# Constant products in TensorE's gaps, a reordered prologue, unscaled row transposes and mask tiles among the projections

## The chip, the cores and the metric

One core of a Trainium2 chip runs the kernel. The metric is the time on the device in microseconds (us), lower is better. The engines are TensorE (PE; its weight loads are PEld), VectorE (DVE), ScalarE (ACT), GpSimd (POOL) and SyncE (SP, which issues DMAs). A profile is one execution; its rows are in us from the first instruction.

## The reference

Two layers, each followed by adding its input and a layer norm, on `x` of 2 x 4096 x 256 in f32:

```python
# layer 1: a gated linear recurrence over the sequence
a = tanh(x @ WA.T); b = x @ WB.T                 # 16 states
g = sigmoid(x @ Wg.T + bg); dx = x @ WD.T + bD
h_t = a_t * h_{t-1} + b_t                        # scan over 4096 tokens
x = layernorm(x + (h @ WC.T) * g + dx * (1 - g))
# layer 2: a transformer block on a chosen eighth of the tokens
w = x @ router_w + router_b
sel = sort(the 511 highest w of each batch)      # threshold: the 512th
x_s, pos, m = x[sel], position_ids[sel], mask[sel][:, sel]
hn = rmsnorm(x_s) * ln1
q, k, v = rope(hn @ wq), rope(hn @ wk), hn @ wv  # 16 heads of 16
x1 = x_s + softmax(q k^T / 4 + m) v @ wo
x2 = x1 + gelu((rmsnorm(x1) * ln2) @ w1) @ w2    # w1: 256 x 1024
out[sel] = x2 * w[sel]; out += x * (1 - (w > threshold))
x = layernorm(x + out)
```

## The kernel before

The program is written out by hand: each engine has its own list of instructions in order, and counting semaphores (`wait_ge`, `then_inc`) order them against each other. Nothing is scheduled by a planner; on each engine an instruction waits for all that stand before it.

**Prologue (lines 411 to 427, 709 to 731, 1051 to 1114, 1375 to 1407).** SP loads the first four groups of `x` and the gate weights; ACT issues the loads of WA, WB, three copies of WC side by side, and the biases. All seven weight loads count on one semaphore, `w_loaded`, and PE waits for all of them (line 711) after turning the first half of the first `x` group. PE then transposes WA and WB (line 714) and the tripled WC (line 717) together, then the second half of `x` (line 664), then Wg and WD (line 723). ACT and DVE split each result into a high and a low part for exact-enough fp32r products.

**Layer 1 (lines 732 to 743, 1408 to 1428).** 16 groups of 512 tokens. Per group PE transposes `x` (`transposes`), forms the recurrence inputs (`recurrence_inputs`), and the gates with the h part last (`gates`, lines 689 to 705). ACT does copies, tanh, sigmoid and the final normalisation, DVE the scan (line 1299) and statistics, POOL a subtraction and the powers.

**Selection (lines 745 to 784, 1356 to 1511).** The 512th-highest logit is found digit by digit: `compare` on DVE (line 1360) marks logits at or above 15 candidates, `count` on PE (line 748) sums over the partitions with eight small products of a matrix of ones, `narrow` on DVE takes the digit. Eight rounds per batch, the two batches interleaved. Then `flag_sums`, `slots` (ranks) and `one_hots` (lines 1457 to 1466: a one-hot of the high part of the slot, one of the low part, and the second times 15 values). `pick_rows` multiplies the one-hots to give the row numbers; `pick_rest` does the other 13 values: the factors of each row (`wf_sel`) and positions. `rows` on DVE makes three index tiles and POOL's `gather_x` and `gather_mask_rows` fetch rows of `x` and of the mask by them; POOL waits for all three index tiles (`rows_ready`, 3).

**Projections (lines 819 to 854, 1005 to 1026).** `first_normalised` on DVE (line 1544) multiplies a gathered chunk of 128 rows by its norm factor `wf_sel[..., 2]`; PE transposes it (line 826), ACT copies it to `hnT` (line 1150), PE forms q and k (line 848) and v (line 852), ACT copies q and k out (line 1160), DVE v (line 1562). PE also turns eight 128 x 512 tiles of mask rows per batch (line 797), which ACT negates and copies (line 1170), SP stores and POOL gathers again by column. In PE's list all eight tiles of batch 0 stand between the projections of batch 0 and those of batch 1, and all eight of batch 1 after the first two chunks of batch 1. `turn_split` (line 867) then turns the split q and k.

**Attention and feed-forward, per batch (lines 1028 to 1047).** PE goes through 64 head units (lines 898, 911, 926), then the output product, the transposes of the normalised rows (`turn_hn`, line 834), the hidden layer (lines 978 and 984) and the second product (line 1001). Before `turn_hn` DVE sums squares and POOL takes the power (line 584), and PE has nothing to do. For batch 0, PE turns the second batch's mask columns there (line 816).

The scratch tiles of the selection lie in `qk[0]` (`scratch`, line 228).

## Time and profile before

| | us |
|---|---|
| median of 3 runs (516.37 to 517.21) | 516.37 |
| the profiled execution, its own time | 516.65 |
| its span, first to last instruction | 514.9 |
| PE busy | 428.7 (83%) |
| DVE busy | 393.8 (76%) |
| ACT busy | 289.9 (56%) |
| POOL busy | 173.5 (34%) |

The 1.75 us between the execution's own time and its span lie outside the instructions. The clock column of the profile (PEclk) is the TensorE clock that was granted, as a share of 2.4 GHz; 0.5 is 1.2 GHz, the lower of its two levels. The mean over the span is 0.934.

### The profile page before, as it was taken

What the parts mean: (1) busy time and instruction counts of PE and PEld (TensorE: products, weight loads), DVE (VectorE), ACT (ScalarE), POOL (GpSimd) and SP (SyncE); (2) the same over time, 40 slices, a digit from 0 to 9 for tenths busy, and PEclk for the clock granted to TensorE, in tenths of its full rate; (3) what the DMA queues carried; (4) which work ended last, traced back from release to release, by engine and by line L of the source; (5) the groups of instructions that cost most, each with busy time, mean ns of one, the idle gap of its engine ahead of it and who ended that gap; (6) DMA issues with size and microseconds to landing.
All of it is one profiled execution on the core that took longest, in us unless ns stands there. A gap on an engine that the chain in (4) does not pass through costs nothing.

```text
span 514.9 us, 9944 instructions
## 1 busy us (share of the span) xinstructions
PE 428.7 (83%) x3394; PEld 326.8 (63%) x3394; DVE 393.8 (76%) x1218; ACT 289.9 (56%) x613; POOL 173.5 (34%) x210
## 2 busy tenths in 40 slices
PE   3598999998999723589887999997998999996970
PEld 2487888776888512457565666665885666664860
DVE  1777898789888788777468999978667999967150
ACT  2344655554465534014687999964577999962200
POOL 9146757756775750354234000001000000000532
PEclk9999999998999955579999999998999999998995
DMA  8613252243222120056670000000000000000110
GB/s 250 215 43 83 83 158 89 81 137 110 81 83 83 41 82 1 26 181 210 237 232 16 3 3 1 3 2 1 0 1 2 2 2 3 2 2 1 35 37 11
DMA packets 29913, 33.90 MB, mean 66 GB/s; under 512 B 6404, under 2 KB 25512, under 8 KB 29864
## 3 DMA queue, kind: packets, MB, share of 16 engines
q1 hardware_dynamic: 23088, 24.78, 14.6%
q0 software_dynamic: 3520, 8.40, 5.5%
q10 hardware_dynamic: 3256, 0.10, 0.4%
q8 instruction: 27, 0.44, 0.4%
q14 instruction: 22, 0.18, 0.1%
HBM read 19.63 MB, written 13.63 MB: 65 GB/s over the span
## 4 chain that ended last, share of the span: by engine, by line
PE 37%; DVE 14%; issue 14%; POOL 9%; ACT 5%; POOLq 1%; DVEq 0%; ACTq 0%
PE ps L911 8%; PE ps L926 5%; PE ps L898 4%; PE ps L1001 4%; PE ps L978 3%; POOL arena L499 3%; PE ps L848 2%; PE ps L867 2%; PE ps L762 2%; POOL r L508 2%; ACT arena L1207 1%; PE ps L984 1%; POOL h_parts L558 1%; POOL rq L513 1%; PE ps L852 1%
## 5 line engine op out<-in xcount | busy, mean ns | idle before, releaser
L1207 ACT ACTIVATE arena<-arena,nmax 128x511 f32<-128x511 f32 x128 | 91.5, 719 | 5.4 <-DVE nmax L1643 5.3
L1643 DVE CUSTOM_DVE_ANT_0 arena<-ps,nmask 128x511 f32<-128x511 f32 x128 | 84.8, 684 | 0.2 <-DVE nmask L1591 0.2
L911 PE MATMUL ps<-ident,arena 128*128 128x128 f32 x512 | 78.7, 276 | 3.6 <-ACT big L403 2.3
L911 PEld LDWEIGHTS ps<-ident,arena 128*128 128x128 f32 x512 | 58.7, 140 | 25.3 <-ACT arena L1207 15.1
L689 PE MATMUL ps<-wgd_hi,x_hi 128*128 128x512 f32 x128 | 51.6, 403 | 0.0
L691 PE MATMUL ps<-wgd_hi,x_lo 128*128 128x512 f32 x128 | 50.5, 394 | 0.0
L690 PE MATMUL ps<-wgd_lo,x_hi 128*128 128x512 f32 x128 | 50.3, 393 | 0.0
L898 PE MATMUL ps<-arena 96*128 96x512 bf16 x128 | 48.5, 385 | 1.9 <-DVE nmask L1591 1.1
L403 DVE COPY big<-ps 128x512 f32<-128x512 f32 x64 | 44.1, 689 | 4.8 <-PE ps L911 3.6
L499 POOL TENSOR_TENSOR arena<-arena 128x512 f32<-128x512 f32 x32 | 41.4, 1294 | 12.4 <-DVE arena L1311 10.8
L403 ACT COPY big<-ps 128x512 f32<-128x512 f32 x64 | 36.9, 577 | 8.0 <-PE ps L926 6.3
L1094 ACT ACTIVATE ob_sb<-arena,nb,rq 128x256 f32<-128x256 f32 x64 | 33.1, 591 | 8.6 <-POOL nb L517 8.5
L1286 DVE TENSOR_TENSOR x_lo<-ps,x_hi 128x512 fp32r<-128x512 f32 x32 | 22.0, 688 | 15.5 <-ACT x_hi L1065 15.5
L664 PE MATMUL ps<-ident,arena 128*128 128x128 f32 x128 | 20.9, 289 | 12.5 <-DVE x_lo L1286 7.6
L1065 ACT CAST x_hi<-ps 128x512 fp32r<-128x512 f32 x32 | 18.6, 580 | 21.2 <-PE ps L664 20.9
L1306 DVE TENSOR_TENSOR arena<-ps,arena 128x512 f32<-128x512 f32 x32 | 21.9, 685 | 10.2 <-PE ps L705 10.1
L1077 ACT ACTIVATE arena<-ps 128x512 f32<-128x512 f32 x32 | 19.2, 599 | 18.0 <-PE ps L698 16.0
L1086 ACT CAST h_parts<-arena 48x512 fp32r<-48x512 f32 x16 | 9.9, 621 | 33.2 <-DVE arena L1299 33.2
L631 POOL COPY arena<-v_sb 128x256 f32<-128x256 f32 x4 | 1.6, 397 | 80.2 <-PE ps L926 80.2
L1001 PE MATMUL ps<-w_sb,big 128*128 128x256 f32 x128 | 28.6, 380 | 0.0
L1319 DVE BATCH_NORM_STATS2 stats<-arena 128x6 f32<-128x256 f32 x64 | 23.9, 415 | 5.8 <-POOL arena L499 5.8
L508 POOL TENSOR_TENSOR r<-v,minus_half 128x8 f32<-128x8 f32 x16 | 26.3, 1643 | 5.9 <-DVE v L1336 5.9
(243 smaller groups left out, 1005.0 us busy)
## 6 DMA issues: line engine op xcount, KB each, us to landing
arena<-in_L_attn_x SPq DMA_DIRECT2D x16, 512.0 KB, 4.6
out<-ob_sb SPq DMA_DIRECT2D x16, 512.0 KB, 3.2
w_sb<-in_L_ffn_w SPq DMA_DIRECT2D x2, 1024.0 KB, 10.3
mt_scratch<-nmask SPq DMA_DIRECT2D x8, 256.0 KB, 4.9
mt_scratch<-big SPq DMA_DIRECT2D x8, 256.0 KB, 4.4
big<-in_L_attn_Wg SPq DMA_DIRECT2D x1, 256.0 KB, 4.2
big<-in_L_attn_WD SPq DMA_DIRECT2D x1, 256.0 KB, 5.5
wqk<-in_L_ffn_wq SPq DMA_DIRECT2D x1, 256.0 KB, 7.7
```

The source lines that it names most:

```text
L403: copy(prT[c % 2][:, h, :, :], ps[:, 2 + u % 2, :].rearrange("p (k n) -> p k n", k=C)).then_inc(prT_copied[u % 2], 1)
L499: pool.tensor_tensor(s, s, u_sb[q][:, :, :], ALU.subtract).then_inc(s_ready, 1)
L508: pool.tensor_tensor(r2[:, :, b, n], v2[:, :, b, n], minus_half[:, 0:2 * T].rearrange("p (k t) -> p k t", k=2), ALU.pow).then_inc(r2_ready, 1)
L689: pe.matmul(o, hi, wgd_hi[:, c, :], start=(c == 0), stop=False)
L690: pe.matmul(o, hi, wgd_lo[:, c, :], start=False, stop=False)
L691: pe.matmul(o, lo, wgd_hi[:, c, :], start=False, stop=False)
L898: pe.matmul(ps[:, S_BANKS[u % AHEAD], :], qkT[0][:, hg * HG + h:hg * HG + h + 1, c * P:(c + 1) * P], qkT[1][:, hg * HG + h:hg * HG + h + 1 ...
L911: mm = pe.transpose(ps[:, 2 + u % 2, k * P:(k + 1) * P], pr[u % 4][:, k * P:(k + 1) * P], ident[:, :])
L1001: mm = pe.matmul(second_out(b, c), hidden_sb[:, f, c * P:(c + 1) * P], w2_sb[:, f, :], start=(f == 0), stop=(f == FB - 1))
L1094: last = act.activation(ob_sb[G % 2][:, t, :], s_sb[G % 2][:, t, :], ACT.Identity, bias=nb[G % 2][:, t:t + 1], scale=rq[:, b, n.start + t: ...
L1207: act.activation(pr[u % 4][:, 0:K - 1], sm[u % 4][:, 0:K - 1], ACT.Exp, bias=nmax[:, c, h:h + 1], scale=-1.0, accum_out=rsum[:, c, h:h + 1 ...
L1643: dve.tensor_tensor_reduce(sm[u % 4][:, 0:K - 1], ps[:, S_BANKS[u % AHEAD], 0:K - 1], nmask[b][:, c, 0:K - 1], 1.0, 3.4e38, ALU.add, ALU.m ...
```

## The change

`fill(bank, n)` is new on PE: n products of a matrix of ones with 512 constant columns into a bank that nobody reads. 14 smaller ones stand in the prologue. The loads get a semaphore each; WC is loaded once and tripled by a DVE copy; PE takes WA and WB as soon as they are there and WC after the first recurrence inputs. ACT makes a one-column copy at the start and issues the bias loads after its first copy of `x`. In `one_hots` the two values that `pick_rows` needs come first. POOL waits for one index tile at a time. `first_normalised` is gone: PE transposes the gathered rows as they are, and the factor is applied in the copies of q, k and v. The mask tiles of batch 0 are dealt out 3, 2, 3 among the first projections of batch 1, and banks are given out anew (`X_BANK`, three banks for mask tiles). The scratch tiles move to `v_sb[1]` and `x_sel[1]`.

```diff
@@ scratch tiles, banks
-            return early_qk[:, at:at + n].bitcast(dt)
+            tile, at = (v_sb[1], at) if at < 992 else (x_sel[1], at - 992)
+            return tile[:, :, :].rearrange("p c d -> p (c d)")[:, at:at + n].bitcast(dt)
-        R_BANK, REST_BANK = (2, 0), (4, 1)
+        R_BANK, REST_BANK = (2, 0), (1, 1)
+        X_BANK = ((2, 3), (3, 3))
@@ POOL
-            pool.wait_ge(rows_ready[0], 3)
...
             def kept(b):
-                pool.wait_ge(hn_ready[b], C)
+                pool.wait_ge(angle_ready[b], 1)
                 for c in range(C):
+                    pool.wait_ge(x_sel_in[b][c], 16)
...
-            gather_x(0)
-            gather_mask_rows(0)
-            pool.wait_ge(rows_ready[1], 3)
-            gather_x(1)
-            gather_mask_rows(1)
-            gather_mask_columns(0)
-            gather_mask_columns(1)
+            for b in range(B):
+                pool.wait_ge(rows_ready[b], 1)
+                gather_x(b)
+                pool.wait_ge(rows_ready[b], 2)
+                gather_mask_rows(b)
+            for b in range(B):
+                pool.wait_ge(rows_ready[b], 3)
+                gather_mask_columns(b)
@@ PE
+            ones_wide = ones_b[:, :].rearrange("p (o n) -> p o n", o=1).broadcast_to((P, 4, P))
+            def fill(bank, n):
+                for _ in range(n):
+                    pe.matmul(ps[:, bank, :], ones_b[:, :], ones_wide, start=True, stop=True)
...
             pe.wait_ge(ident_ready, 2)
+            ident_bits = ident[:, :].bitcast(BF16)
+            for n in range(10):
+                pe.matmul(ps[:, 7, 0:2 * P], ident_bits[:, 0:P], ident_bits, start=True, stop=True)
             transposes(0, 0)
-            pe.wait_ge(w_loaded, 16 * 7)
+            pe.wait_ge(wab_loaded, 16 * 2)
...
-            for h in range(2):
-                mm = pe.transpose(ps[0:HROWS, 5, h * P:(h + 1) * P], wc_raw[:, h, :], ident[:, :])
-            mm.then_inc(wt_done, 1)
+            mm.then_inc(w_turned, 1)
+            for n in range(4):
+                pe.matmul(ps[:, 7, 0:2 * P], ident_bits[:, 0:P], ident_bits, start=True, stop=True)
             transposes(0, 1)
+            pe.wait_ge(wgd_loaded, 16 * 2)
...
             pe.wait_ge(split_ready, KD)
             recurrence_inputs(0)
+            pe.wait_ge(split_ready, KD + 1)
+            for h in range(2):
+                mm = pe.transpose(ps[0:HROWS, 5, h * P:(h + 1) * P], wc_raw[:, h, :], ident[:, :])
+            mm.then_inc(w_turned, 1)
             for c in range(KD):
                 transposes(1, c)
...
             def pick(b, lo, hi, bank, at, signal):
-                pe.wait_ge(lo_ready[b], 1)
+                pe.wait_ge(lo_ready[b], 1 if hi == 2 else 2)
...
             def pick_rest(b):
+                if b > 0:
+                    pe.wait_ge(angle_ready[b - 1], 1)
                 pick(b, 2, VALS, REST_BANK[b], 0, rest_picked)
 
-            for r in range(4):
+            pe.wait_ge(pool_const, 9 + 2 * B)
+            pe.wait_ge(t_ready, 2 * NGB)
+            fill(7, 6)
+            for r, gap in enumerate((13, 10, 4, 7)):
                 count(0, r)
+                fill(7, gap)
             for r in range(4, ROUNDS):
                 count(1, r - 4)
+                fill(7, 2)
                 count(0, r)
+                fill(7, 2)
             count(1, 4)
+            fill(7, 1)
             flag_sums(0)
+            fill(7, 2)
             count(1, 5)
+            fill(7, 13)
             count(1, 6)
+            fill(7, 12)
             pick_rows(0)
             count(1, 7)
             pick_rest(0)
             flag_sums(1)
+            fill(7, 12)
...
             def turn_first_hn(b, c):
-                pe.wait_ge(hn_ready[b], c + 1)
-                if c + b * C >= 2:
-                    pe.wait_ge(hnT1_ready[(c + b * C - 2) // C], (c + b * C - 2) % C + 1)
-                if b > 0:
-                    pe.wait_ge(mT_ready[b - 1], MS // P)
+                pe.wait_ge(x_sel_in[b][c], 16)
+                if b == 0 and c >= 2:
+                    pe.wait_ge(hnT1_ready[0], c - 1)
+                elif b == 1:
+                    pe.wait_ge(hnT1_ready[1], c)
...
-            turn_mask_rows(0)
-            for c in range(2):
+            turn_mask_rows(0, range(3))
+            turn_first_hn(1, 0)
+            project(1, range(1))
+            turn_mask_rows(0, range(3, 5))
+            turn_first_hn(1, 1)
+            project(1, range(1, 2))
+            turn_mask_rows(0, range(5, 8))
+            for c in range(2, C):
                 turn_first_hn(1, c)
-            for c in range(2):
-                project(1, range(c, c + 1))
-                turn_first_hn(1, 2 + c)
-            turn_mask_rows(1)
+            turn_mask_rows(1, range(8))
+            pe.wait_ge(v_ready[1], 2)
+            fill(7, 10)
+            pe.wait_ge(hnT1_ready[1], C)
             pe.wait_ge(mT_ready[1], MS // P)
...
                 if b == 0:
                     turn_second_mask_columns()
-                    pe.wait_ge(nm_ready[1], 2)
+                    pe.wait_ge(nm_ready[1], C)
+                    fill(5, 5)
+                else:
+                    fill(5, 14)
                 turn_hn(b)
@@ ACT
-            for r in range(3):
-                act.dma_start(wc_raw[:, :, r * N:(r + 1) * N], WC.rearrange("(h e) n -> e h n", e=P)).then_inc(w_loaded, 16)
-            act.wait_ge(bias_zeroed, 1)
...
+            act.dma_start(wc_one[:, :, :], WC.rearrange("(h e) n -> e h n", e=P)).then_inc(wc_loaded, 16)
+            act.wait_ge(ident_ready, 3)
+            act.copy(nb[0][:, 0:1], minus_half[:, 0:1])
...
             copy_xT(0, 0)
+            load_biases()
             copy_xT(0, 1)
-            act.wait_ge(wt_done, 1)
-            act.copy(wc_hi[:, :], ps[0:HROWS, 5, 0:D]).then_inc(wt_copied, 1)
             for c in range(KD):
...
+            act.wait_ge(w_turned, KD + 2)
+            act.copy(wc_hi[:, :], ps[0:HROWS, 5, 0:D]).then_inc(w_hi_ready, 1)
...
             def copy_qk(b, c):
-                act.copy(qk[b][:, c, :], ps[:, 4 + c % 2, :]).then_inc(qk_ready[b], 1)
+                act.wait_ge(angle_ready[b], 1)
+                act.mul(qk[b][:, c, :], ps[:, 4 + c % 2, :], wf_sel[:, b, c, 2:3]).then_inc(qk_ready[b], 1)
...
-            sines(0)
             for c in range(2):
                 copy_first_hnT(0, c)
+            sines(0)
...
             copy_qk(0, C - 1)
+            copy_mask_rows(0, range(3))
+            copy_first_hnT(1, 0)
+            copy_qk(1, 0)
+            copy_mask_rows(0, range(3, 5))
+            copy_first_hnT(1, 1)
+            more_parts(0, 0)
+            copy_qk(1, 1)
+            copy_mask_rows(0, range(5, 8))
+            for c in range(2, C):
+                copy_first_hnT(1, c)
+            copy_mask_rows(1, range(5))
+            more_parts(0, 1)
+            copy_mask_rows(1, range(5, 8))
             sines(1)
...
@@ DVE
             rest_of_x(0, 0)
-            dve.wait_ge(wt_done, 1)
+            dve.wait_ge(w_turned, 1)
...
-            rest_of_x(0, 1)
             for m in range(2):
...
+            rest_of_x(0, 1)
+            dve.wait_ge(wc_loaded, 16)
+            dve.tensor_copy(wc_raw.rearrange("p h (r n) -> p h r n", r=3),
+                            wc_one.rearrange("p h (r n) -> p h r n", r=1).broadcast_to((P, 2, 3, N))).then_inc(split_ready, 1)
...
             def one_hots(b):
-                dve.tensor_tensor(at_hi[:, b], slot_b[:, b, 0:1, :].broadcast_to((P, P, NT)), hi_rep[:, :, :],
-                                  ALU.is_equal).then_inc(at_ready[b], 1)
                 step.link(dve.tensor_tensor(
                     at_lo[:, b], slot_b[:, b, 1:2, :].broadcast_to((P, C, NT)),
...
+                place(0, 2)
+                dve.tensor_tensor(at_hi[:, b], slot_b[:, b, 0:1, :].broadcast_to((P, P, NT)), hi_rep[:, :, :],
+                                  ALU.is_equal).then_inc(at_ready[b], 1)
                 dve.wait_ge(parts_ready[b], 1)
+                place(2, VALS)
...
             def value(b, c):
                 dve.wait_ge(v_done[b], c + 1)
-                dve.tensor_copy(v_sb[b][:, c, :], ps[:, 6 + c % 2, 0:D]).then_inc(v_ready[b], 1)
+                dve.tensor_scalar(v_sb[b][:, c, :], ps[:, 6 + c % 2, 0:D], wf_sel[:, b, c, 2:3], None,
+                                  ALU.mult).then_inc(v_ready[b], 1)
```

`place(v0, v1)` multiplies the low one-hot by the values v0 to v1 - 1 and signals `lo_ready`. The calls of `first_normalised` are removed from DVE's list.

## Rows read from the trace of the kernel before

**Rows 1.** The page, slices of the whole span (one slice is 12.9 us).

```profile
PE   3598999998999723589887999997998999996970
...
PEclk9999999998999955579999999998999999998995
```

**Rows 2.** Busy us by stretch: length, PE, PEld, DVE, ACT, POOL, clock, DMA share, GB/s.

```profile
181.00:225.00 44.00, 18.37 (x196) 14.09 (x197) 36.99 (x172) 11.01 (x20) 14.93 (x19) 0.50 0.19 61
354.00:358.00 4.00, 3.95 (x13) 2.85 (x14) 3.90 (x12) 2.33 (x3) 0.15 (x1) 0.57 0.01 4
470.00:474.00 4.00, 4.00 (x13) 2.88 (x14) 2.65 (x7) 2.46 (x3) 0.00 (x0) 0.57 0.02 4
239.70:258.10 18.40, 14.27 (x89) 10.64 (x88) 11.05 (x28) 13.86 (x32) 3.97 (x5) 1.00 0.75 254
```

**Rows 3.** The timeline of 0 to 25 us: start, duration, engine, line, operation.

```profile
4.84 1.09 PE L664 MATMUL ps<-ident,arena 128*128 128x128 f32 x4 [4.84 <-DMA arena<-in_L_attn_x]
...
5.12 1.28 ACT L1065 ACT_TABLE_LOAD   x1 [5.12 <-issue]
...
7.03 0.69 DVE L1286 TENSOR_TENSOR x_lo<-ps,x_hi 128x512 fp32r<-128x512 f32 x1 [3.71 <-ACT x_hi L1065]
...
9.94 0.61 PE L714 MATMUL ps<-ident,nmask 16*128 16x16 f32 x4 [4.01 <-DMA nmask<-in_L_attn_WC]
...
11.74 1.71 PE L723 MATMUL ps<-ident,big 128*128 128x128 f32 x8
...
14.47 0.50 PE L675 MATMUL ps<-x_hi,wab_hi 128*128 128x512 f32 x1 [1.02 <-DVE wab_lo L1383]
...
14.81 0.40 PE L676 MATMUL ps<-x_lo,wab_hi 128*128 128x512 f32 x1
...
17.85 1.27 DVE L1299 TENSOR_TENSOR_SCAN arena<-arena,zero_state,ps 48x512 f32<-48x512 f32 x1
...
23.14 0.70 PE L698 MATMUL ps<-wc_d,h_parts 128*128 128x512 f32 x2 [1.67 <-DVE wc_d L1402]
```

**Rows 4.** DMA issues of 0 to 20 us: KB each, median us to landing.

```profile
nmask<-in_L_attn_WC ACTq DMA_DIRECT2D x3, 16.0 KB, 6.1
...
nmask<-in_L_attn_WB ACTq DMA_DIRECT2D x1, 16.0 KB, 3.7
```

**Rows 5.** The timeline of 197 to 215 us, selection.

```profile
197.03 0.58 PE L748 MATMUL ps<-arena,ones_b 128*128 128x60 bf16 x8 [0.70 <-DVE arena L1360]
...
198.10 0.58 PE L748 MATMUL ps<-arena,ones_b 128*128 128x60 bf16 x8 [0.48 <-DVE arena L1360]
...
206.15 2.28 DVE L1458 TENSOR_TENSOR arena<-slot_b,qk 128x4096 bf16<-128x4096 bf16 x1
...
208.66 1.16 DVE L1464 TENSOR_TENSOR arena<-at_lo,qk 128x1920 bf16<-128x1920 bf16 x1
...
209.88 2.22 PE L762 MATMUL ps<-arena 128*128 128x8 bf16 x32 [3.02 <-DVE arena L1464]
...
214.00 1.22 POOL L579 DMA_INDIRECT x_sel<-out,row_x  x1 [22.89 <-DVE row_t L1477]
```

**Rows 6.** The timeline of 220 to 259 us, projections and mask tiles.

```profile
220.94 1.12 PE L826 MATMUL ps<-ident,hn 128*128 128x128 f32 x4 [5.05 <-DVE hn L1544]
...
222.19 3.22 PE L848 MATMUL ps<-wqk,hnT 128*128 128x512 f32 x4
...
231.26 1.88 PE L848 MATMUL ps<-wqk,hnT 128*128 128x512 f32 x4
...
254.03 4.02 ACT L1170 ACTIVATE big<-ps 128x512 f32<-128x512 f32 x8
...
258.10 1.99 PE L867 MATMUL ps<-ident_b,arena 128*96 128x128 bf16 x32 [1.29 <-ACT big L1170]
```

**Rows 7.** The timeline of 469 to 476 us, before the second feed-forward.

```profile
469.92 2.12 PE L834 MATMUL ps<-ident,hn 128*128 128x128 f32 x8 [3.77 <-DVE hn L1537]
...
474.79 1.09 PE L984 MATMUL ps<-hnT_lo,w_hi 128*128 128x512 f32 x4
```

More of the change, by code:

```diff
@@ L241, in build @@
         rope_a, rope_b = (arena2[:, n * 1024:(n + 1) * 1024].rearrange("p (c n) -> p c n", c=2) for n in range(2))
-        v_sb = [sb(f"v_sb{b}", [P, C, D]) for b in range(B)]
         e_rest = arena2[:, 4096:5120].rearrange("p (e n) -> p e n", e=2)
@@ L1246, in _ @@
             copy_qk(0, C - 1)
-            sines(1)
-            copy_mask_rows(0)
-            for c in range(2):
-                copy_first_hnT(1, c)
-            more_parts(0, 0)
-            for c in range(2):
-                copy_first_hnT(1, 2 + c)
-                copy_qk(1, c)
-            more_parts(0, 1)
-            copy_mask_rows(1)
+            copy_mask_rows(0, range(3))
[11 more added lines that the diff above has]
+            copy_mask_rows(1, range(5, 8))
+            sines(1)
             for c in range(C):
@@ L1724, in _ @@
             slots(1)
-            for c in range(2):
-                first_normalised(0, c)
             one_hots(1)
-            for c in range(2, C):
-                first_normalised(0, c)
             cosines(0)
@@ L1740, in _ @@
                     parts(0, 0)
-                if c == 2:
-                    for n in range(C):
-                        first_normalised(1, n)
             parts(0, 1)
```

86 lines of the change are left out of this document (43 added, 43 removed).

## The prediction

> **What bounds the kernel now.** I read the slices of the page first, for the clock: it is at 0.5 in one long stretch, 181 to 225 us, and falls for a moment near 126, 355 and 471 us; PE shows nines nearly everywhere else [rows 1]. The busy times by stretch then say who works where. In layer 1 PE is full, so what starts earlier in the prologue is kept to the end. In 181 to 225 us PE is busy 18.4 of 44 us at clock 0.50 while DVE is busy 37.0: the selection is DVE's [rows 2]. Next the timeline at its start, for what PE waits on: it stands 4.01 us for a DMA of WC [rows 3], which is three small loads of 6.1 us each, the last issued on ACT's queue behind WA and WB [rows 4]. Then the timeline of the selection and of the projections, for the chain one-hots, picked rows, gather, normalised rows, transposes [rows 5, 6], and last the gap before the second feed-forward [rows 7].
>
> All of it is worked against the profiled execution: 516.65 us (span 514.9), 0.28 above the median of 516.37.
>
> **Part 1, prologue.** WB takes 3.7 us against 6.1 for WC [rows 4], so with a semaphore of their own WA and WB (first on ACT's queue) are there when the first transposes end, at 4.84 + 1.09 = 5.9 us. ACT's 1.28 us table load, which ran at 5.12 to 6.4 and held up the first copy, goes to ACT's empty time ahead of 4.8 by the one-column copy: 0.4 us. The first rest of x ended at 7.03 + 0.69 = 7.7; now about 7.3, and the second half of `x`, which was turned just ahead of the transposes at 11.74, is turned then, 3.5 us earlier [rows 3]. From there: transposes to 8.4, ACT's copy to 9.05 (0.6), DVE's rest to 9.8 (0.69). The WA/WB split (about 1.1 us in four small DVE operations) now runs while PE turns `x`; before it stood behind the rest of x and released line 675 at 14.47. Wg and WD are turned meanwhile (1.71 us at most), to 10.1. So line 675 starts near 10.1: 4.4 us earlier. Given back: the two WC transposes and their copy now stand between that and the second group (about 0.6). The scan at 17.85 becomes 14.1, the h part of the first gates at 23.14 becomes 19.4, if the bias loads, now issued on ACT behind its first copy (from 6.5 instead of 3.5 us), land before about 17.5. Sum -3.7. Bounds: 0 (a load I moved is late and takes the whole of it) and -4.4. ACT's four bias issues, some 1.6 us, fit between its copies at 6.5 and 8.4; the tripling copy on DVE is about 0.2 us, beside PE.
>
> The row that bears on the clock: from 9.94 to 13.3 us PE ran transposes and nothing else; they came 0.21 us apart (8 in 1.71), which is the low level, and at 14.81 the products last 0.40 as they do later at the full one [rows 3]. So transposes alone raised the clock here. The Trainium skill (TensorE: Matmul & The Clock Gate, Part 4: PE-mode transpose) says that the full clock does not engage for transposes; the trace does not agree. By that rule only the 14 small products would count and the first recurrence inputs would run at half clock, a rival below.
>
> **Part 2, products that fill gaps.** No row shows one; the nearest is line 984: four of 512 columns in 1.09 us of which the last alone is 0.40, so (1.09 - 0.40) / 3 = 0.23 us each at full clock [rows 7], 0.46 at the low one. In the count rounds two counts are 1.07 us apart and PE idles 0.48 of that [rows 5]. One count (0.58 low, about 0.4 full) and two fills (0.46) take 0.86 at full clock: nothing waits, and nothing is gained either, since DVE sets the pace; at the low clock they take 1.50 and are late by 0.43. The runs of 13, 12 and 12 are 3.0, 2.8 and 2.8 us; the idle they fill ahead of count(1,6) and of the picked rows is about 3.3 and 3.0 [rows 5]. The six ahead of the first count (1.4 us from 178.4) delay it by some 0.5 us, and DVE reads it 2 us later. I take 0 for the lot, bounds -0.3 and +1.0; what a warm clock gives comes in part 4.
>
> **Part 3, one-hots and index tiles.** The big one-hot takes 2.28 us, the values 1.16, then the pick starts at 209.88 [rows 5]. Now only 2 of 15 values stand ahead: 1.16 x 13/15 = 1.0 less, one more operation (0.3) more; the pick starts 0.7 earlier, near 209.2. POOL's gather at 214.00 waited for the third index tile, row_t; two small DVE operations (0.35) less. First gather near 212.9, -1.1. The other 13 values run on DVE beside the pick (2.2 us) and cost nothing.
>
> **Part 4, rows transposed unscaled, warm.** The first transposes at 220.94 waited for DVE, which did angles and slots before it scaled the rows [rows 6]; the rows themselves are there by 212.9 + 1.2 + some 3 = 217. Now PE takes them when its 12 fills end, near 217.9. Projection 0 took 3.22 for its first part at the low clock against 1.88 at the full one, 1.3 less [rows 6]. So the first chunk is done 4.5 us earlier; then PE waits for the second batch's one-hots on DVE, whose list is eight scalings shorter but was never waiting for PE, and the last chunk of batch 0 ends about 236.6 instead of 239.7: -3.1. Scaling in the copies is the same operation with a factor: 0, bounds -0.1 and +0.1 each over 16. The added waits: `copy_qk` waits for the angles, which DVE has some 3 us before the first q and k and 5 us before those of batch 1 (behind it on ACT stand the next hnT copies, for which PE would wait); `pick_rest(1)` waits for the angles of batch 0, long done; POOL's `kept` waits for rows that PE has turned by then. All 0.
>
> **Part 5, mask tiles.** From the last copy of batch 0 to the end of the tiles (239.7 to 258.1) ACT is busy 13.9 of 18.4 us [rows 2]; its last eight tiles, 0.50 each, end what `turn_split` at 258.10 waits for [rows 6]. ACT's list is the same work in another order, plus the second batch's sines. It waits 4.5 us now. In the new order it waits for projection (1,0), which stands behind three tiles (2.1), for tiles 3 and 5 behind projections (0.7, 0.5), for the first tile (0.7) and little else; with the last three tiles behind `more_parts` I get about 5.4. So of the 3.1, 2.2 are left: `turn_split` at 255.9. The ten fills there (2.3 us) end near 255.1, under ACT's tiles. Stores of batch 0 end some 4 us later than now, but its columns are gathered well before PE wants them near 270. Bounds: +1 and -3.5. What follows to 275 us is unchanged.
>
> **Part 6, feed-forwards.** Batch 1: PE is idle 3.77 us up to 469.92, then 4 us at clock 0.57 [rows 2, 7], that is 4 x 0.43 = 1.7 us lost. 14 fills are 3.2 us, they end before 469.9. The transposes are still held by DVE's rows and ACT's copy; I take -1.3, bounds 0 and -1.7. Batch 0: five fills (1.2 us) start only when ACT has copied the last mask tile, 353.9, so `turn_hn` starts about 1 us later, against a low clock over 354 to 358 [rows 2]. If the clock holds, -0.4; if it falls all the same, +1.5. I take 0.
>
> **Sum.** -3.7 - 2.2 - 1.3 = -7.2 on 516.65: 509.45, and 0.28 less for the median, 509.2. Attention and layer 1 are PE bound and unchanged.
>
> **Rivals.**
> A. The prologue is held by another load (biases, or the one WC): parts 2 to 6 alone, 512.9. For: WC's loads took 6.1 us each against 3.7 for WB, so the queues are full there [rows 4]; against: every load but the biases moves forward. Chance 0.12.
> B. The middle keeps its end, since ACT waits longer among interleaved tiles: 511.4. For: ACT ends last there; against: everything ahead of it is 3 us earlier. 0.15.
> C. The prologue runs at the low clock until after the first recurrence inputs: six products at 0.43 instead of 0.23, +1.4, 510.6. The row on transposes speaks against it. 0.13.
> D. Slower: constant products do not hold the clock in the selection. It decides from the first long gap, 180 us on: eight rounds late by 0.43 (3.4), 13 and 12 fills at 0.46 against gaps of 3.3 and 2.3 (2.7 and 3.2), 12 after the flag sums (2.5), 14 at 466 (2.7), five at 354 (1.5): +16, less the prologue's 3.7 and 0.7 of part 3, 528. For: no row shows what such a product does to the clock; against: every stretch in which PE is dense has clock 1.0. 0.06; smaller mishaps of this kind that end above before 0.02.
> E. Gains and losses cancel: 516.4. 0.04.
> The forecast itself has 0.48, with its own range 507.5 to 510.3.
>
> **How the numbers follow.** Within 0.2% (515.3 to 517.4) is what a measurement of this kernel can't tell from no change. Faster: 0.48 + 0.12 + 0.15 + 0.13 = 0.88; same 0.04; slower 0.08. The range leaves out D and E and reaches to A: 505.8 to 513.4.
>
> **What would show it.** Right: line 675 starts near 10.1, the h part of the first gates near 19.4; PEclk is 1.0 from 180 to 260; the first gather starts near 212.9 - 3.7, `turn_split` near 255.9 - 3.7; clock 1.0 at 470. Wrong: PE's count waits for nothing while DVE waits for it in the rounds (D); line 698 waits for a DMA (A); ACT's tiles end at 254 or later (B).

## The result, and the profile after

| | before | after |
|---|---|---|
| median, in turn on the same chip | 516.79 (4 runs, 516.37 to 517.92) | 510.54 (4 runs, 509.67 to 513.3) |
| the profiled execution, its own time | 516.65 | 513.3 |
| its span | 514.9 | 511.4 |
| PE busy | 428.7 | 457.1 |
| mean granted clock | 0.934 | 0.97 (0.97 to 0.98 over the four) |

The ratio of the two kernels' runs is 0.9867 (95% interval 0.9839 to 0.9895), that of the two medians alone 0.9879: the kernel after is 1.2 to 1.3% faster. 509.2 was forecast, with 505.8 to 513.4 as the range. The profiled execution is the slowest of the four, 2.8 above the median, so all that it shows is read beside the others below.

The page's slices of the kernel after (40 of the whole span, 12.8 us each) are to be held against [rows 1]:

```profile
PE   7698999997999877998997999998998999998970
...
PEclk9899999999999999799999999998999999999995
```

The long stretch of fives is gone, and a 7 is left at slice 17. The windows of the kernel after, in the columns of [rows 2], say where the clock is still low:

```profile
22.00:24.00 2.00, 0.91 (x5) 0.94 (x6) 1.29 (x2) 1.97 (x3) 0.00 (x0) 0.74 0.01 4
24.00:26.00 2.00, 2.00 (x6) 1.61 (x6) 1.36 (x2) 0.72 (x2) 0.98 (x1) 0.50 0.00 0
...
177.00:210.00 33.00, 26.59 (x248) 12.88 (x249) 28.21 (x134) 10.19 (x19) 8.49 (x13) 1.00 0.10 33
210.00:217.90 7.90, 7.90 (x46) 4.92 (x46) 5.49 (x34) 0.00 (x0) 5.03 (x6) 0.57 0.22 67
218.00:260.00 42.00, 38.53 (x259) 27.89 (x258) 25.92 (x68) 24.05 (x50) 16.53 (x15) 1.00 0.69 228
...
351.00:354.00 3.00, 3.00 (x11) 1.86 (x10) 2.90 (x10) 0.08 (x1) 0.00 (x0) 0.50 0.00 0
...
470.00:474.00 4.00, 3.78 (x17) 2.81 (x16) 3.93 (x13) 2.31 (x3) 0.00 (x0) 1.00 0.00 0
```

The selection (177 to 210) runs at 1.00 where it had 0.50. New falls stand at 23 to 26 and at 210 to 217, and the one before the first feed-forward has moved from 354 to 351. At 470, where 0.57 stood, it is 1.00. A fall near 126 us is in both kernels and costs nothing that shows: "no five" below has it and "both" has not, and their first compares stand at 175.78 and 175.77.

The timeline of the kernel after, 0 to 21 us, against [rows 3]:

```profile
8.31 4.16 POOL L483 IOTA qk<- 128x4096 bf16 x1
...
8.55 1.91 PE L738 MATMUL ps<-ident,big 128*128 128x128 f32 x8
...
9.41 0.69 DVE L1335 TENSOR_TENSOR x_lo<-ps,x_hi 128x512 fp32r<-128x512 f32 x1 [0.84 <-ACT x_hi L1108]
...
10.02 2.53 DVE L1435 COPY nmask<-nmask 128x96 f32<-128x96 f32 x1
10.25 0.77 PE L686 MATMUL ps<-x_hi,wab_hi 128*128 128x512 f32 x1
10.27 2.28 DVE L1439 TENSOR_TENSOR wgd_lo<-ps,wgd_hi 128x512 fp32r<-128x512 f32 x2
...
10.81 0.63 PE L687 MATMUL ps<-x_lo,wab_hi 128*128 128x512 f32 x1
...
12.52 0.48 PE L688 MATMUL ps<-x_hi,wab_lo 128*128 128x512 f32 x1
...
12.84 0.38 PE L746 MATMUL ps<-ident,nmask 128*48 128x128 f32 x2
...
14.93 1.27 DVE L1348 TENSOR_TENSOR_SCAN arena<-arena,zero_state,ps 48x512 f32<-48x512 f32 x1
...
20.21 0.70 PE L709 MATMUL ps<-wc_d,h_parts 128*128 128x512 f32 x2 [1.65 <-DVE wc_d L1455]
```

The recurrence inputs start at 10.25 (before: 14.47), but the middle four last 0.63 each, the low level. The copy that triples WC, which I had at 0.2, takes 2.53 and ends with POOL's iota (8.31 + 4.16 = 12.47).

The timeline of the kernel after from the selection to the projections, against [rows 5, 6]:

```profile
196.50 0.40 PE L767 MATMUL ps<-arena,ones_b 128*128 128x60 bf16 x8 [0.23 <-DVE arena L1409]
196.74 0.59 PE L666 MATMUL ps<-ones_b 128*128 128x512 bf16 x2
197.57 0.39 PE L767 MATMUL ps<-arena,ones_b 128*128 128x60 bf16 x8 [0.24 <-DVE arena L1409]
...
204.91 2.75 PE L666 MATMUL ps<-ones_b 128*128 128x512 bf16 x12
207.50 2.26 PE L781 MATMUL ps<-arena 128*128 128x8 bf16 x32
...
211.34 1.22 POOL L583 DMA_INDIRECT x_sel<-out,row_x  x1 [21.81 <-DVE row_t L1535]
...
213.20 4.87 PE L666 MATMUL ps<-ones_b 128*128 128x512 bf16 x12
217.91 0.60 PE L857 MATMUL ps<-ident,x_sel 128*128 128x128 f32 x4
218.85 1.96 PE L879 MATMUL ps<-wqk,hnT 128*128 128x512 f32 x4 [0.33 <-ACT hnT L1194]
...
234.46 0.69 ACT L1205 ACTIVATE qk<-ps,wf_sel 128x512 f32<-128x512 f32 x1 [5.21 <-PE ps L879]
...
254.70 1.96 PE L898 MATMUL ps<-ident_b,arena 128*96 128x128 bf16 x32 [0.32 <-issue]
```

The counts are faster (0.40 for 0.58) and still 1.07 us apart: DVE sets the pace. Twelve constant products take 2.75 at full clock (0.23 each) and 4.87 behind the flag sums, nearly all of them at the low one.

The timeline of the kernel after, before each feed-forward, against [rows 7]:

```profile
350.71 2.31 PE L666 MATMUL ps<-ones_b 128*128 128x512 bf16 x5 [2.15 <-ACT nmask L1317]
352.82 1.63 PE L865 MATMUL ps<-ident,hn 128*128 128x128 f32 x8
...
463.77 3.19 PE L666 MATMUL ps<-ones_b 128*128 128x512 bf16 x14
467.70 1.55 PE L865 MATMUL ps<-ident,hn 128*128 128x128 f32 x8 [0.74 <-DVE hn L1595]
...
471.53 1.10 PE L1015 MATMUL ps<-hnT_lo,w_hi 128*128 128x512 f32 x4
```

**The stages side by side.** From each trace I took seven landmarks: the first `compare`, the turning of the split q and k, the last copy of the head outputs and the first GELU of each batch, the last scatter. The table has the us between them, one profiled execution per kernel:

| stage | before | after | again | no product | gap | no five | both | both, tiles together |
|---|---|---|---|---|---|---|---|---|
| 1 to first compare | 178.86 | 177.49 | 176.94 | 176.24 | 175.60 | 175.78 | 175.77 | 175.81 |
| 2 to split q, k | 79.24 | 77.21 | 77.15 | 76.90 | 77.58 | 76.63 | 76.58 | 76.00 |
| 3 attention 0 | 89.19 | 89.38 | 89.39 | 89.96 | 89.39 | 89.38 | 89.97 | 89.53 |
| 4 to first GELU, batch 0 | 12.24 | 13.22 | 13.28 | 12.63 | 13.18 | 11.83 | 11.82 | 11.84 |
| 5 to end of attention 1 | 103.89 | 103.90 | 103.89 | 103.90 | 103.90 | 103.88 | 103.88 | 103.89 |
| 6 to first GELU, batch 1 | 12.04 | 11.00 | 11.00 | 12.26 | 11.00 | 10.99 | 11.00 | 11.00 |
| 7 to last scatter | 26.98 | 26.96 | 26.98 | 26.97 | 26.98 | 26.95 | 26.96 | 26.98 |
| own time | 516.65 | 513.30 | 512.75 | 512.94 | 511.73 | 509.74 | 509.93 | 509.02 |

The kernel after won 1.37 in stage 1, 2.03 in stage 2 and 1.04 in stage 6, and lost 0.98 in stage 4 and 0.19 in stage 3.

### The profile page after: what moved, and what is told of

It reads as the page before. It is cut to its first block, busy times and chain, and to the rows that moved or that the text cites. A ratio compares the mean times of both kernels' runs of the same rounds, so it can differ in the third digit from the quotient of the medians.

```text
span 511.4 us, 10221 instructions
## 1 busy us (share of the span) xinstructions
PE 457.1 (89%) x3533; PEld 336.6 (66%) x3533; DVE 393.8 (77%) x1213; ACT 290.8 (57%) x614; POOL 173.4 (34%) x210
## 4 chain that ended last, share of the span: by engine, by line
PE 46%; DVE 12%; POOL 9%; issue 7%; ACT 6%; POOLq 1%; DVEq 0%; ACTq 0%
PE ps L942 11%; PE ps L957 7%; PE ps L929 6%; PE ps L1032 4%; POOL arena L503 3%; PE ps L1009 3%; PE ps L879 3%; PE ps L666 2%; PE ps L898 2%; PE ps L781 2%; POOL r L512 2%; PE ps L905 1%; ACT arena L1252 1%; PE ps L1015 1%; POOL h_parts L562 1%
## 5 line engine op out<-in xcount | busy, mean ns | idle before, releaser
L666 PE MATMUL ps<-ones_b 128*128 128x512 bf16 x125 | 33.6, 409 | 3.0 <-ACT nmask L1317 2.1
```

What stands on the lines that cost most here:

```text
L666: pe.matmul(ps[:, bank, :], ones_b[:, :], ones_wide, start=True, stop=True)
```

## The experiments

Twelve kernels ran: the kernel after once more, and eleven edits of it. Each left one trace, so a stage's time is that of one execution. The first four shared a chip (kernel before there: 517.63), the next four another (518.16), the last four a third (517.87). The kernel after, unchanged, ran only on the first of these chips.

**The kernel after, unchanged** ("again").

> The changed kernel itself, once more, as the reference of the others on this chip and as a second profile. In the first profile (execution of 513.3 us, the slowest of four; the others 509.7 to 511.2) the clock fell at 23 us, just after the start of layer 1, and the second scan came 12.36 us after the first against 10.86 before: 1.5 us of the prologue's 2.9 lost. Theory 1 (chance): whether the clock falls there differs from one execution to the next; a profile near 510 us shows the two scans about 10.9 apart, and executions spread by 2 to 4 us. Theory 2 (fixed): the new prologue makes the clock fall there always; every profile shows 12.4.

Median 512.26 (509.89 to 514.59), ratio 0.9903 (0.9869 to 0.9937). Unchanged, the same program took anything from 509.7 to 514.6 (both sets together), and the mean clock goes along in part: 0.977 at 509.89, 0.970 or 0.971 at the three slowest. It can't be all of it, as 512.75 and 514.59 both have 0.970, and the kernel before took from 515.7 to 519.8 on this chip at 0.934 every time. The fall at 23 us is in this trace too, that at 351 as well: theory 2 is not refuted here. That part of each is chance, the next runs show.

**No constant product at all.**

```diff
-                for _ in range(n):
+                for _ in range(0):
```

and likewise for the 14 small ones of the prologue.

> The changed kernel without any of the added products (none in the prologue, the selection, before the split or before the feed-forwards); order, waits and loads stay. Theory 1 (order carries most): fills give the second feed-forward 1.0 and the first projection 0.7 to 1.3 and take 1.0 in the first feed-forward, so this is 0.5 to 2 us slower than the changed kernel, near 511.5. Rival (the clock carries most of the gain): it loses 4 us or more and ends at 514 or above. The clock is 0.5 from about 180 to 223 us again, and the pace of the counts stays at 1.07 us.

Median 514.57 (512.85 to 517.65, 12 runs), ratio 0.9955 (0.9931 to 0.9979). So of the 5.4 us that the kernel after was ahead on this chip (517.63 to 512.26), about 2.3 hang on the products and 3.1 on the order of the work; the intervals of the two ratios just overlap (0.9931 and 0.9937 are their inner ends), so the split is rough. It lies between theory 1 (0.5 to 2) and the rival (4 or more). Where? The stage from the first compare to the split is not slower without them: 76.90, against 77.15 in "again". This window of the run without products shows DVE busy 18.2 of 20 us while PE is at 0.50:

```profile
188.00:208.00 20.00, 8.22 (x115) 6.44 (x116) 18.23 (x84) 6.45 (x10) 0.41 (x2) 0.50 0.08 27
```

Against the execution of "no five" below (509.74), in which the clock held nearly throughout, the run without products loses 0.46 in stage 1, 0.27 in stage 2, 0.58 in stage 3, 0.80 in stage 4 and 1.27 in stage 6, 3.4 in all, against 3.2 in their own times. The 0.58 of stage 3 is no work of the products: the clock fell at 272 us in this run, and it did so in "both" below too, which has all of them and takes 89.97 there. The largest piece is the second feed-forward; the 106 products between 177 and 254 us, most of the 125 of this kind, bring 0.3.

**The prologue of before under the rest of after.** PE, ACT and DVE have the old order up to the first recurrence inputs.

> The changed kernel with the prologue of before (one semaphore for seven loads, WC loaded three times, table load late, bias issues first, old order on PE and DVE, no products there); all the rest changed. Theory 1: the prologue is worth the 2.9 us that the first scan came earlier, less what the clock's fall at 23 us costs, so this takes 1.5 to 3 us more than the changed kernel: 512 to 513.5. Rival: the prologue's gain is all given back in layer 1 (the clock), then the same time within 0.5 us.

Median 514.08 (511.89 to 517.61), ratio 0.9932 (0.9907 to 0.9957): the new prologue is worth 1.8 us against the unchanged kernel on that chip, inside theory 1's 1.5 to 3, though the intervals overlap. The first recurrence input is at 14.22, the scan at 17.58. The profiled execution is the slowest of nine (517.61), and the clock fell in it at 24.4 us, for twice as long as in "after": its first compare is at 181.11, later than before. So the fall at the start of layer 1 is not the new prologue's own.

**Products in the gaps of the first group** ("gap").

```diff
+                if G == 0 and q == 0:
+                    pe.wait_ge(pool_const, 2)
+                    fill(7, 6)
                 if G == 0:
                     pe.wait_ge(split_ready, 2 * KD + 2)
...
+                if G == 0:
+                    pe.wait_ge(h_ready, 1)
+                    fill(2, 5)
                 if G + 2 < NGB:
                     transposes(G + 2, 1)
```

> The changed kernel with six more constant products after the first group's gate products (PE waits there 1.7 us for the constants) and five before the second half of group 2 is turned (1.5 us idle). Theory 1 (those two idles let the clock fall at 23 us in some executions): it stays 1.0 from 13 to 120 us, the second scan comes 10.9 us after the first in every profile, the median falls by 0.5 to 1.5 us and the spread shrinks. Rival (the fall has nothing to do with these gaps): same median, or 0.3 us more for products that are late.

Median 509.99 (509.56 to 511.76), ratio 0.9862 (0.9834 to 0.989), 2.3 below the unchanged kernel on the same chip (the intervals overlap a little), where theory 1 gave 0.5 to 1.5. In the windows of this run the clock holds where it had fallen:

```profile
22.00:24.00 2.00, 1.59 (x10) 1.07 (x8) 1.35 (x3) 1.97 (x3) 0.00 (x0) 1.00 0.06 15
24.00:26.00 2.00, 2.00 (x10) 1.61 (x9) 1.68 (x3) 0.98 (x2) 1.20 (x1) 1.00 0.00 0
```

and the first two scans are 10.83 us apart, against 12.22 for the unchanged kernel. In "after" and "again", and in the two runs below with four products and with the tiles together, PE waited for the h part and for x with nothing to do (1.72 busy of 18 to 22 us in "again") and the clock fell; in the five kernels with products in these gaps it did in none. In "no product", "no five" and "early" it held without them. So whether it falls is chance, and the products seem to take the chance away; five traces against seven make that likely and no more. The times say the same: none of the 14 executions of "gap", "both" and "both, tiles together" took over 511.8, while 10 of the 28 of "after", "again", "no five", "early" and the first run with the tiles together took over 512.

**Batch 0 without its five products** ("no five").

```diff
-                    pe.wait_ge(nm_ready[1], C)
-                    fill(5, 5)
+                    pe.wait_ge(nm_ready[1], 2)
```

> Batch 0's feed-forward starts as in the kernel before: the five products are gone and PE waits for two mask tile copies, not four. Theory 1: the five products cost what they take at the low clock, because it falls while PE waits for ACT's last tile copy and they start after that. Last output product of batch 0 to first GELU is 13.2 us after the change and 12.2 before; here 12.2 to 12.4, time -0.9 us. Theory 2: the wait for the last tile copy is what costs, and the products themselves little: with only the products gone this was 12.6, so here again 12.2, but of the 1.0 us 0.4 belongs to the wait and 0.6 to the products. The two give the same time here and are told apart by this run beside the one without any products. Rival: the later start of the transposes is hidden by DVE's and ACT's chain on the normalised rows: stays at 13.2, time the same.

Median 510.3 (509.74 to 513.54), ratio 0.9877 (0.9842 to 0.9913). Stage 4 took 11.83, less than the 12.2 that both theories gave, as the clock did not fall in this stage at all. Theory 2's 0.4 for the wait is out by another trace: in "no product", which waits for all four tile copies, the transposes start 6.75 behind the last copy of the head outputs, as they do before. The rest, 12.63 there for 12.24, goes with its fall, which comes 1.1 later and so lies less over the transposes and more over the hidden layer.

**The five products earlier** ("early").

```diff
-                    pe.wait_ge(nm_ready[1], C)
-                    fill(5, 5)
+                    pe.wait_ge(ms_ready, 1)
+                    fill(0, 5)
+                    pe.wait_ge(nm_ready[1], 2)
```

> In batch 0 the five products stand ahead of PE's wait for the normalised rows (they start when the sum of squares' inputs are there) and not behind the wait for the last mask tile copy. Theory 1: they fill the idle time, the clock does not fall at 350.6 and the transposes and the hidden layer run at 1.0: last output product to first GELU 11.0 to 11.6 as in batch 1 after the change (11.0), against 13.2; time -1.6 to -2.2 us. Rival 1: the clock falls all the same (the second batch's mask columns turned there are no dense work), then 12.2 to 12.4, -0.9. Rival 2: the transposes are bound by DVE's rows, and nothing changes but the clock: 12.6, -0.6.

Median 509.91 (509.65 to 513.2), ratio 0.9872 (0.9836 to 0.9908). The timeline of this run:

```profile
347.17 1.25 PE L666 MATMUL ps<-ones_b 128*128 128x512 bf16 x5 [0.54 <-DVE ms L1579]
348.90 1.60 PE L865 MATMUL ps<-ident,hn 128*128 128x128 f32 x8 [0.48 <-DVE hn L1596]
```

The products sit in the gap and stage 4 takes 11.83 again. It took 11.83 in a third run too, the next one, which has the five products where the kernel after has them. So 11.83 is what the stage takes at full clock, wherever the products stand. What the products decide is the price of a fall: 12.24 (before) and 12.63 (no product) without them, 13.22, 13.28 and 13.18 with five behind it, since they run at 0.46 each in front of the transposes. Whether "early" keeps the clock up or only had luck, its one trace cannot say. The last four runs, all with it, showed no fall there either: none in five traces, against seven in the nine others.

**Four products, not twelve, behind the second flag sums.**

```diff
-            fill(7, 12)
+            fill(7, 4)
```

> Four constant products behind the second batch's flag sums, not twelve. In the kernel after they took 4.87 us at clock 0.5 (213.2 to 218.07) and the gathered rows were transposed at 217.9. Theory 1: they hold PE while the rows are there: the first transposes start at 215.5 to 216 (counted in that run's time), the first chunks 1.5 to 2 us earlier; at the end of the projections 0.5 to 1.0 us is left, as PE then waits for the second batch's one-hots on DVE. Time -0.7. Rival: with fewer products the clock stays at 0.5 longer (it rose to 1.0 just behind the twelve), projection 0 takes 3.2 and not 1.9 us, and nothing is left or 0.5 us is lost. Theory 3: the rows arrive only at 217.5 and nothing changes.

Median 514.07 (512.12 to 514.82), ratio 0.9916 (0.9885 to 0.9946): slower than the three other kernels on this chip by 3.2 to 4.2 us, where theory 1 gave -0.7 and the rival 0.5 at most. The clock fell at 22 us here too, for 6.8 us (stage 1: 178.44). The rows are transposed 3.53 behind the first gather instead of 6.57, but stage 2 takes 79.27:

```profile
222.04 2.19 PE L781 MATMUL ps<-arena 128*128 128x8 bf16 x32 [2.01 <-DVE arena L1521]
224.09 3.76 PE L879 MATMUL ps<-wqk,hnT 128*128 128x512 f32 x4
```

PE comes early to the second batch's one-hot, waits 2.01, the clock falls, and a projection takes 3.76 for 1.96. How much of this is the edit's doing is asked again below.

**Batch 0's mask tiles together**, ahead of batch 1's projections, as before; rows still transposed unscaled.

```diff
-            turn_mask_rows(0, range(3))
-            turn_first_hn(1, 0)
-            project(1, range(1))
-            turn_mask_rows(0, range(3, 5))
-            turn_first_hn(1, 1)
-            project(1, range(1, 2))
-            turn_mask_rows(0, range(5, 8))
+            turn_mask_rows(0, range(8))
+            for c in range(2):
+                turn_first_hn(1, c)
+                project(1, range(c, c + 1))
```

ACT's copies follow.

> The mask tiles of batch 0 stand together ahead of batch 1's projections, as in the kernel before; rows are still transposed unscaled. Theory 1: dealing them out is what makes the middle shorter: without it ACT has no work beside PE's transposes and projections of batch 1 and eight tiles at the end: first compare to turning of the split q and k 79 us against 77.15, time +1.5 to +2. Theory 2 (part 4 of the prediction, and its part 5, where dealing out gives 0.9 back): the gain of 2.0 comes from the rows turned earlier, and the order itself costs or is nothing: 76.3 to 77.2, time -0.8 to 0.

Median 510.92 (510.15 to 514.01), ratio 0.9868 (0.9839 to 0.9896). Stage 2 took 77.39, with the clock at 0.90 over 230 to 234 and 0.68 over 234 to 238, where "after" has 1.00. Theory 1 (79) is out, though this trace can't say what the order costs at an even clock.

**Both gap edits** ("both": "gap" and "early" together), then each of the last three edits on top of it, so that the falls elsewhere do not blur them.

> The kernel after with both edits that kept PE at work in a gap: six and five constant products at the start of layer 1, and batch 0's five ahead of the wait for the normalised rows. Theory 1: what spread the executions of the kernel after (509.7 to 514.6) is whether the clock falls at 23 us (worth 1.5) and at 351 us (worth 1.4); where it held at both, the profiled execution took 509.74. Here it holds at both: 509.6 to 510.0 in nearly all executions, highest below 511. Rival: other falls that no profile has shown make the upper level (513.2 in two of six of the run before, 511.7 in two of five), and it stays: median near 510, highest above 511.5.

Median 510.14 (509.77 to 510.74), ratio 0.985 (0.9816 to 0.9885). The level did not get below the best executions of the kernel after (509.67), but the spread shrank from 4.7 us over six runs ("again") to 1.0 over four. That is theory 1, except that two of the four lie above the 509.6 to 510.0 that it gave for nearly all. Four executions are few, and the low clock doesn't explain every slow one: in "early" 513.20 and 513.18 stand at a mean clock of 0.975, beside 509.93 at 0.977.

> As the kernel with both gap edits, with four products and not twelve behind the second batch's flag sums. In the run with four, PE then waited 2.01 us for DVE's one-hot at 220 us and the clock fell from 223 to 230: the stretch from first gather to the turning of the split q and k took 45.4 us against 43.3. Theory 1: that is the edit's own doing (PE gets to the wait earlier, so the wait is longer), and it shows again: time +2 against the kernel with both gap edits. Rival: it was the chance of one execution: the difference is within 0.5, as the six executions' median of 514.07 came from the two other places where the clock falls.

Median 511.37 (510.6 to 512.44), ratio 0.9876 (0.9848 to 0.9905): +1.2 against "both", so the twelve seem worth having (six executions against four, intervals overlapping; theory 1 gave 2, the rival 0.5), but by another place than I expected. PE waited only 0.75 at 219 us; the clock fell behind the second `pick_rest`:

```profile
226.87 3.42 PE L787 MATMUL ps<-arena 128*128 128x52 bf16 x32
230.11 3.38 PE L885 MATMUL ps<-wqk,hnT 128*128 128x512 f32 x4
```

The clock fell within a few us of there in the first kernel with the tiles together, in the one with the old prologue and in the last run below too, all three with the twelve, and not in "both" or "after", which run the same products there: the earlier arrival makes a fall likelier at best.

> As the kernel with both gap edits, with batch 0's mask tiles together ahead of batch 1's projections. With the kernel after this stretch took 43.6 us against 43.3 (one execution each). Theory 1: the order is worth 0.3 us at most. Rival (dealing out is the gain of the middle): +1.5 to +2.

Median 509.57 (509.02 to 510.44), ratio 0.9842 (0.9812 to 0.9872), the lowest median of all versions. Stage 2 is 0.58 shorter than in "both", with a fall of equal length in each, and the medians are 0.57 apart. The profiled executions are 0.91 apart; 0.44 of that is stage 3, where the clock fell in "both". So dealing the tiles out gains nothing and seems to cost half a microsecond, with the sign of theory 1 turned round; the executions of the two overlap (509.77 to 510.74 and 509.02 to 510.44). Against the kernel after's 0.9867 the intervals overlap; the medians of the two (on different chips) are 1.0 apart.

> As the kernel with both gap edits, with POOL's 4.16 us iota of the high one-hot's pattern moved from the prologue (8.3 to 12.5 us) to the end of layer 1. Theory 1: DVE's copy that triples WC took 2.53 us and the low part of Wg and WD 2.28 (1.28 for two of them in the kernel before) because POOL works beside them; without it the copy takes 0.2 to 0.5 and the low part 0.64 to 1.3. The first recurrence inputs wait for neither, so the first scan stays at 14.7; the first gates are held by other work and the time changes by 0 to -0.5. Rival: the DVE operations are long for their own sake (the copy reads with a stride of zero), and stay. Rival 2: the first gates wait for them, time -1.

```diff
-            pool.iota(hi_rep[:, :, :], [[1, P], [0, NT]], ...).then_inc(pool_const, 1)
...
+                if G == NGB:
+                    pool.iota(hi_rep[:, :, :], [[1, P], [0, NT]], ...).then_inc(hi_made, 1)
```

Median 511.57 (511.46 to 513.65), ratio 0.9874 (0.984 to 0.9909): 1.4 slower than "both", where theory 1 gave 0 to -0.5 (four executions each; those of the two don't overlap). Its timeline has both ends of the matter:

```profile
9.84 0.20 DVE L1444 COPY nmask<-nmask 128x96 f32<-128x96 f32 x1
...
10.09 0.69 DVE L1448 TENSOR_TENSOR wgd_lo<-ps,wgd_hi 128x512 fp32r<-128x512 f32 x1
...
12.32 0.38 PE L751 MATMUL ps<-ident,nmask 128*48 128x128 f32 x2
...
14.42 1.27 DVE L1357 TENSOR_TENSOR_SCAN arena<-arena,zero_state,ps 48x512 f32<-48x512 f32 x1
...
184.46 4.17 POOL L573 IOTA qk<- 128x4096 bf16 x1
...
184.87 3.79 DVE L1402 TENSOR_SCALAR Wf<-Wf,rb_col 128x32 f32<-128x32 f32 x1
```

In the prologue the copy takes 0.20 for 2.53 and the low parts 0.69 each, as theory 1 had it. The scan comes at 14.42 and the first compare at 175.18, which is 0.6 earlier than in "both" and 3.68 earlier than before. (Theory 1 left the scan at 14.7; that miss is answered by the next block.) But the iota in its new place holds an operation of DVE for 3.79 us (184.87 + 3.79 = 188.66; the iota ends at 188.63) that takes 0.29 in "both":

```profile
185.47 0.29 DVE L1400 TENSOR_SCALAR Wf<-Wf,rb_col 128x32 f32<-128x32 f32 x1
```

The first gather comes 37.2 behind the first compare instead of 33.8. The place was badly chosen; the cause is shown twice.

"Both" adds what the low clock had hidden. In its trace the recurrence inputs ran at the full level:

```profile
9.36 3.19 DVE L1442 COPY nmask<-nmask 128x96 f32<-128x96 f32 x1
...
9.59 0.47 PE L686 MATMUL ps<-x_hi,wab_hi 128*128 128x512 f32 x1 [0.62 <-DVE x_lo L1342]
9.90 0.39 PE L687 MATMUL ps<-x_lo,wab_hi 128*128 128x512 f32 x1
...
12.60 0.40 PE L749 MATMUL ps<-ident,nmask 128*48 128x128 f32 x2 [1.39 <-DVE wgd_lo L1446]
```

They ended at 11.2, 1.8 us earlier than in "after" (12.52 + 0.48), and the scan still came at 14.71: PE waited 1.39 for DVE, which the iota held until 12.5. In all eleven traces with this prologue and the iota in it the copy ends at 12.54 or 12.55, though it starts anywhere from 9.36 to 10.15. What the prologue is worth with neither the iota nor the low clock, no run shows: with the iota away the first inputs ran at the low level to the fourth of the six.

## Why the prediction was right

The median is 1.3 above the forecast, well inside the range; most of the mechanism is as predicted. That the sum comes so near is partly luck, as its terms missed in both directions.

- **Part 1** (-3.7). Line 675's products came at 10.25 (forecast near 10.1), no load was late (rival A is out: line 709, the former 698, waits for DVE). The h part came at 20.21, not 19.4: -2.9. The failed step is "the tripling copy on DVE is about 0.2 us, beside PE": it took 2.53 to 3.19, and with the iota away, the first compare moved by -3.68. Rival C (whose price is 6 x 0.20 = 1.2 and not the 1.4 given) happened in part: in the profiled execution the first inputs ran at the low level to the last of the six. But the scan was at 14.71 or 14.72 in nine traces with this prologue, whether full speed began with the first product ("no five", "both") or with the fifth ("again"), as the copy was the later of the two; only here (14.93) and without the small products (15.18) did the low level show. That transposes alone can raise the clock stands: in the trace of before the last two of the eight at line 723 (11.74 to 13.45) take 0.32 and 0.27, the others 0.42. But when they do is no sure thing: in "no product" PE transposed from 7.49 to 10.1 without a gap and all six inputs behind it were still at the low level.
- **What part 1 left out.** Layer 1 keeps what the prologue wins only if the clock stays up. In the profiled execution it fell at 23 us, which made the first two scans 12.36 apart instead of 10.86, so 1.37 of 2.92 was left. That gap was already in the kernel before, and the clock held in its profiled execution (1.00 over 22 to 30). This is the largest piece by which the profiled execution (513.30) lies above the forecast; what it is of the median's 1.3, no run shows.
- **Part 2** (0). Right: 0.23 us a product, first compare to first gather 33.85 with them and 33.97 without. The step "PEclk is 1.0 from 180 to 260" failed between 210.7 and 217.5: the clock fell during the picks and the twelve products took 4.87, not the 2.8 given. Rival D, which was to end at 528, is out. What was said against it, that the clock is 1.0 wherever PE is dense, did not hold in [rows 2] already: 3.95 of 4.00 us busy at 0.57 over 354 to 358.
- **Part 3** (pick -0.7, gather -1.1). Measured from the first compare: pick start 31.02 before, 30.01 after (-1.0); gather 35.14 and 33.85 (-1.3).
- **Part 4** (last copy of q and k of batch 0, -3.1). 60.2 before, 57.0 after, from the first compare: -3.2. The copies with a factor took 0.69 for 0.59 (q, k) and 0.48 for 0.42 (v), inside the bounds.
- **Part 5** (turning at -2.2). -2.03, and -2.61 in "no five", so rival B is out. The share that dealing out gives back was put at 0.9; "both" with the tiles together shows 0.58, one trace against one.
- **Part 6** (batch 1 -1.3, batch 0 taken as 0 with -0.4 and +1.5 as its ends). Batch 1 gave -1.04. Batch 0 had both ends: -0.41 where the clock held, +0.98 where it fell.

In the execution of "no five" (509.74), where neither fall occurred, the stages differ from before by -3.08, -2.61, +0.19, -0.41 and -1.05: -6.9, beside the forecast's -7.2. Its terms there are +0.6 (part 1), -0.4 (part 5), -0.4 (batch 0), +0.25 (batch 1) and +0.19 (stage 3, of which the forecast said that it is unchanged; it is longer in every trace, and why stays open). The median of the kernel after lies 0.8 above this execution. The two falls, each in some executions and not in others, are the likely reason; as only profiled executions show where the clock fell, it is not shown.

The Trainium skill (SBUF — State Buffer, Who interferes with whom) has the rule that I had not applied: a VectorE copy or tensor_scalar in its faster mode and a GpSimd instruction exclude each other for a whole instruction, and the second to start is blocked. The traces agree: the operations of 2.53, 3.19 and 3.79 us each end within 0.1 of the iota. Whether they run in that mode, no row shows. The trace of before could not show the block: DVE had nothing to do from 7.72 to 12.68, all through the iota.

## What to carry to other kernels

Constant products were worth their place where PE itself ends the chain just behind the gap: 14 before a feed-forward gave 1.0 to 1.3 us, 106 in a stage that VectorE bounds 0.3. Put them ahead of the wait for the data and not behind it, where, once the clock has fallen, they run at 0.46 each in front of real work. When a step moves to an earlier time, list what the other engines do at that time, not only the queues: here a 0.2 us copy moved beside a 4.2 us iota.

## What was not expected of the hardware

- **An iota on POOL holds some DVE operations whole.** A copy within SBUF and a small tensor_scalar waited for its end; a subtraction that reads PSUM, issued beside the same iota at 9.41 in the kernel after, took 0.69 as elsewhere. (The two of line 1439, printed with 2.28, stand behind the copy in DVE's list and end with it.)
- **The same program gets different clocks.** With one and the same prologue, full speed began at the first of the six recurrence inputs in "no five" and "both", at the second or third in "early", at the fifth in "again"; the fall at 23 us and that at 351 come and go with the code there unchanged. The Trainium skill (TensorE: Matmul & The Clock Gate, Part 1: The HAM clock gate) says as much of the start of a kernel, where the number of slow products varies from run to run.
- **The printed clock is not reliable at the start.** Over 0 to 14 us the window prints 1.00, while four transposes take 1.09 and later 0.60. There the durations are the thing to read. The trace's own records of the clock start only where those change, at 12.7 in "after" and 5.8 in "both"; what lies ahead of the first record is printed as 1.00.
- **Small products with many weight loads did not hold the clock.** During 32 products of 8 and 32 of 52 columns, each with its own weights, it fell at 210.7 with PE busy throughout (5.80 of 5.80 us ahead of the fall, 204.9 to 210.7, the first 2.75 of them constant products). It fell within 5 us of there in every trace with the constant products. Line 781's 32 products of 52 columns take 3.4 us at either level, so this costs nothing itself, only what comes next.
- **The kernel before spread from 515.7 to 520.8** over the three chips at a mean clock of 0.934 in nearly every run. Its one profile is of 516.65; why others are over 3 us longer at the same clock stays open, and the same may lengthen some executions of the kernels after it.
